# Split down weights kept in device memory: stored at their first use, read back at later ones, in a ring of three pairs

## The reference

```python
x = x + 0.5 * ffn(layernorm(x), ...)
x = x + mamba(layernorm(x), ...)
x = x + 0.5 * ffn(layernorm(x), ...)
# ffn: 8 experts, 128 -> 512 -> 128
h = silu(x @ w_gate[e]) * (x @ w_up[e])
expert_out = h @ w_down[e]
cw = softmax(x @ w_router) * softmax(x @ w_gating / 0.1)
cw = cw / (sum(cw) + 1e-9)
out = sum over e of expert_out[e] * cw[e]
```

## Time and profile before

| | |
|---|---|
| median of 3 runs | 1244.02 us (1243.34 to 1245.47) |
| profiled execution | 1242.44 us, span 1240.6 us |
| granted TensorE clock | 1.00 of full |
| busy: PE, PEld, DVE, ACT, POOL | 1233.1, 1058.2, 1143.4, 1003.6, 446.4 us |
| device memory read, written | 83.30 MB, 2.69 MB |
| DMA moved | 184.84 MB, mean 149 GB/s |

### The profile page before, as it was taken

The page is one execution under the profiler, slowest core; times in us unless marked ns, Lnnn a source line. Parts: engine busy times, 40 slices in busy tenths (PEclk is TensorE's granted clock), DMA queues, the critical chain, the costliest instruction groups (busy, mean ns, idle before and its releaser), DMA issues.

```text
span 1240.6 us, 20186 instructions
## 1 busy us (share of the span) xinstructions
PE 1233.1 (99%) x7072; PEld 1058.2 (85%) x7072; DVE 1143.4 (92%) x1368; ACT 1003.6 (81%) x2122; POOL 446.4 (36%) x571
## 2 busy tenths in 40 slices
PE   9999999999999999999999999999999999999999
PEld 7787788888888888888888888888888888887887
DVE  6958899999999999999999999997999999978877
ACT  7678789798898898988879898797988978846654
POOL 1021134445453463453434434452444344402000
PEclk9999999999999999999999999999999999999999
DMA  8412458888788997987889887986688979932322
GB/s 227 111 27 45 105 116 174 165 171 167 162 176 178 183 187 157 198 170 165 181 180 187 166 196 160 191 181 138 131 166 169 196 169 194 182 63 43 74 48 60
DMA packets 121015, 184.84 MB, mean 149 GB/s; under 512 B 11344, under 2 KB 38096, under 8 KB 120912
## 3 DMA queue, kind: packets, MB, share of 16 engines
q0 software_dynamic: 53568, 97.54, 45.0%
q1 hardware_dynamic: 67344, 86.00, 26.6%
HBM read 83.30 MB, written 2.69 MB: 69 GB/s over the span
## 4 chain that ended last, share of the span: by engine, by line
PE 93%; DVE 3%; ACT 2%; issue 1%; DMA 1%; SPq 0%; DVEq 0%; ACTq 0%
PE PS L1105 28%; PE PS L996 19%; PE PS L999 18%; PE PS L997 18%; PE PS L1101 2%; PE PS L1097 2%; PE PS L1099 2%; PE PS L1163 1%; PE PS L1148 1%; DVE HB L1345 1%; PE PS L1032 1%; DVE HL L1301 1%; PE PS L1040 1%; DMA YE<-CWD 1%; PE PS L1003 0%
## 5 line engine op out<-in xcount | busy, mean ns | idle before, releaser
L1105 PEld LDWEIGHTS PS<-WD,HB 128*128 128x128 f32 x3200 | 393.9, 191 | 22.1 <-issue 2.0
L1105 PE MATMUL PS<-WD,HB 128*128 128x128 f32 x3200 | 395.9, 275 | 0.0
L1345 DVE TENSOR_TENSOR HB<-PS,HB 128x1024 f32<-128x1024 f32 (+1 forms) x336 | 322.9, 962 | 72.5 <-PE PS L999 56.7
L1555 ACT ACTIVATE HB<-PS 128x512 f32<-128x512 f32 x512 | 294.9, 596 | 95.5 <-PE PS L999 93.5
L1733 POOL DMA_DIRECT2D Y<-HS x252 | 221.8, 954 | 317.6 <-DMA Y<-HS 151.7
L996 PE MATMUL PS<-XH,WG 128*128 128x512 f32 x509 | 219.7, 432 | 0.3 <-ACT HB L1555 0.2
L996 PE MATMUL PS<-XH,WU 128*128 128x512 f32 x512 | 204.4, 399 | 0.4 <-DVE HB L1345 0.4
L999 PE MATMUL PS<-XH,WU 128*128 128x512 f32 x512 | 201.2, 393 | 0.0
L999 PE MATMUL PS<-XH,WG 128*128 128x512 f32 x509 | 200.7, 394 | 0.1
L997 PE MATMUL PS<-XH,WU 128*128 128x512 f32 x512 | 200.4, 391 | 0.0
L997 PE MATMUL PS<-XH,WG 128*128 128x512 f32 x509 | 199.3, 392 | 0.0
(11 more groups left out here) (164 smaller groups left out, 1572.9 us busy)
## 6 DMA issues: line engine op xcount, KB each, us to landing
BCB<-BCD SPq DMA_DIRECT2D x128, 512.0 KB, 5.2
Y<-HS POOLq DMA_DIRECT2D x252, 256.0 KB, 6.0
XT<-YE POOLq DMA_DIRECT2D x99, 256.0 KB, 5.1
YE<-CWD SPq DMA_DIRECT2D x27, 256.0 KB, 4.5
AT<-YE POOLq DMA_DIRECT2D x21, 256.0 KB, 3.3
WD<-in_L_ffn_w_down_dram SPq DMA_DIRECT2D x8, 256.0 KB, 6.0
XT<-in_L_attn_x_dram SPq DMA_DIRECT2D x7, 256.0 KB, 5.8
out_dram<-XT SPq DMA_DIRECT2D x7, 256.0 KB, 5.4
```

The costliest lines, as they stand in the source:

```text
L1105: z = pe.matmul(part(g, j), HB[:, i % NH, j * P:(j + 1) * P], WD[:, e, c, :], start=c == 0 and j == 0, stop=c == FC - 1 and j == SUB - 1)
L1345: v.tensor_tensor(H, PS[:, NG + i % 2:NG + i % 2 + n, :], H, ALU.mult).then_inc(S["v_h"], 1)
L1555: a.activation(HB[:, i % NH, :], gate(i), ACT.Silu).then_inc(S["a_sil"], 1)
```

## The change

The 16 pairs that are made for the first time (`MADE`: 10 in position 0, 4 in position 1, 2 in position 14) are still split on ScalarE and VectorE. After the low part, SP stores the split pair, 128 partitions of 2 KB, to a new array `WDD` in device memory (`wd_store`). The 38 later pairs (`READ`) are not split; SP reads them back (`wd_load`) into the ring, which now has three pairs. A read is entered in SP's list when the pair three before it has been multiplied, and after the row loads of experts that come before it. TensorE waits for the read's semaphore instead of those of the two splits. A slot of the ring in which a made pair lies may be written anew only when that pair's store has landed, too.

```diff
+WEIGHTS_RING = 3
+PAIRS_TURNED = [i for i in TURNED_SLOTS if i % PAIR == 0]
+MADE = [i for i in PAIRS_TURNED if not any(k % SLOTS == i % SLOTS for k in PAIRS_TURNED if k < i)]
+READ = [i for i in PAIRS_TURNED if i not in MADE]
...
+    def weight_loads():
+
+        while reads and (asked[0] == len(TURNED) or TURNED[asked[0]] * FC + FC > reads[0] - SPLIT - PAIR - 2):
+            step("wd_load", reads.pop(0))
...
-            if m % PAIR == 0 and m in TURNED_SLOTS:
+            if m in MADE:
                 split_at[m] = split(m)
                 if m not in scalar_splits:
                     step("wd_lo", m, v=.4)
+                    step("wd_store", m)
             m -= 1
             if m in scalar_splits:
                 step("wd_lo", m, after=split_at[m], v=.35)
+                step("wd_store", m)
+            m = nd + SPLIT + PAIR
+            if m in READ:
+                reads.append(m)
             row_loads()
+            weight_loads()
...
-        WDS = sb("WDS", [P, 2, 2, PAIR, P], F32R)
+        WDS = sb("WDS", [P, WEIGHTS_RING, 2, PAIR, P], F32R)
+        WDD = nc.dram_tensor("WDD", [E, FC // PAIR, P, 2, PAIR, P], F32).ap()
...
         def wait_weights_free(eng, i):
-            n = TURNED_SLOTS[i]
-            if n >= 2 * PAIR:
-                eng.wait_ge(S["m_dn"], [k for k in TURNED_SLOTS if TURNED_SLOTS[k] == n - PAIR - 1][0] + 1)
+            n = pair(i) - WEIGHTS_RING
+            if n >= 0:
+                eng.wait_ge(S["m_dn"], PAIRS_TURNED[n] + PAIR)
+                if PAIRS_TURNED[n] in MADE:
+                    wait_weights_stored(eng, PAIRS_TURNED[n])
...
+                elif s[0] == "wd_store":
+                    i = s[1]
+                    wait_weights_high(wt, i)
+                    wt.wait_ge(S["v_wd"], MADE.index(i) + 1)
+                    r = pair(i) % WEIGHTS_RING
+                    sy.dma_start(WDD[i // FC % E, i % FC // PAIR], f32(WDS[:, r])).then_inc(S[f"c_ws{r}"], 16)
+                elif s[0] == "wd_load":
+                    i = s[1]
+                    wait_weights_free(wt, i)
+                    wait_weights_stored(wt, [k for k in MADE if k % SLOTS == i % SLOTS][0])
+                    r = pair(i) % WEIGHTS_RING
+                    sy.dma_start(f32(WDS[:, r]), WDD[i // FC % E, i % FC // PAIR]).then_inc(S[f"c_wl{r}"], 16)
...
-                        wait_weights_high(wt, first)
+                        if first in MADE:
+                            wait_weights_high(wt, first)
+                        else:
+                            wait_weights_read(wt, first)
```

More of the change, by code:

```diff
@@ L445, in row_loads @@
             asked[0] += 1
+    reads = []
+    def weight_loads():
+        while reads and (asked[0] == len(TURNED) or TURNED[asked[0]] * FC + FC > reads[0] - SPLIT - PAIR - 2):
+            step("wd_load", reads.pop(0))
     begun = {"before": 0, "scans": 0, "closing": 0}
@@ L747, in macaron_program @@
             S[n] = ctx.enter_context(nc.semaphore(n))
+        for r in range(WEIGHTS_RING):
+            S[f"c_ws{r}"] = ctx.enter_context(nc.semaphore(f"c_ws{r}"))
+            S[f"c_wl{r}"] = ctx.enter_context(nc.semaphore(f"c_wl{r}"))
         for b in range(BR):
@@ L826, in wait_weights_high @@
             by_scalar = i in scalar_splits
-            same = [k for k in TURNED_SLOTS if k <= i and k % PAIR == 0 and (k in scalar_splits) == by_scalar]
+            same = [k for k in MADE if k <= i and (k in scalar_splits) == by_scalar]
             eng.wait_ge(S["a_wd" if by_scalar else "v_wh"], len(same))
@@ L840, in wait_weights_free, with wait_weights_stored, wait_weights_read @@
         def wait_weights_free(eng, i):
-            n = TURNED_SLOTS[i]
-            if n >= 2 * PAIR:
-                eng.wait_ge(S["m_dn"], [k for k in TURNED_SLOTS if TURNED_SLOTS[k] == n - PAIR - 1][0] + 1)
+            n = pair(i) - WEIGHTS_RING
[3 more added lines that the diff above has]
+                    wait_weights_stored(eng, PAIRS_TURNED[n])
+        def wait_weights_stored(eng, i):
+            r = pair(i) % WEIGHTS_RING
+            eng.wait_ge(S[f"c_ws{r}"], 16 * sum(k <= i and pair(k) % WEIGHTS_RING == r for k in MADE))
+        def wait_weights_read(eng, i):
+            r = pair(i) % WEIGHTS_RING
+            eng.wait_ge(S[f"c_wl{r}"], 16 * sum(k <= i and pair(k) % WEIGHTS_RING == r for k in READ))
         def added(g):
@@ L1091, in _ @@
                     if g in TURNED:
-                        W = WDS[:, pair(i) % 2]
+                        W = WDS[:, pair(i) % WEIGHTS_RING]
                         first = i // PAIR * PAIR
                         high = HI[:, TURNED_SLOTS[i] % HI_RING, :]
-                        wait_weights_high(wt, first)
+                        if first in MADE:
+                            wait_weights_high(wt, first)
+                        else:
+                            wait_weights_read(wt, first)
                         wait_high(wt, i)
                         pe.matmul(turned(g), W[:, 0, c % PAIR, :], high, start=c == 0, stop=False)
-                        wt.wait_ge(S["v_wd"], pair(i) + 1)
+                        if first in MADE:
+                            wt.wait_ge(S["v_wd"], MADE.index(first) + 1)
                         pe.matmul(turned(g), W[:, 1, c % PAIR, :], high, start=False, stop=False)
@@ L1307, in _ @@
                     wt.wait_ge(S[f"c_wd{i // FC % E}"], 16)
-                    v.tensor_copy(WDS[:, pair(i) % 2, 0], WD[:, i // FC % E, c:c + PAIR, :]).then_inc(S["v_wh"], 1)
+                    v.tensor_copy(WDS[:, pair(i) % WEIGHTS_RING, 0], WD[:, i // FC % E, c:c + PAIR, :]).then_inc(S["v_wh"], 1)
                 elif k == "wd_lo":
@@ L1312, in _ @@
                     wait_weights_high(wt, i)
-                    v.tensor_tensor(WDS[:, pair(i) % 2, 1], WD[:, i // FC % E, c:c + PAIR, :], f32(WDS[:, pair(i) % 2, 0]),
+                    v.tensor_tensor(WDS[:, pair(i) % WEIGHTS_RING, 1], WD[:, i // FC % E, c:c + PAIR, :], f32(WDS[:, pair(i) % WEIGHTS_RING, 0]),
                                     ALU.subtract).then_inc(S["v_wd"], 1)
@@ L1571, in _ @@
                     wt.wait_ge(S[f"c_wd{i // FC % E}"], 16)
-                    a.activation(WDS[:, pair(i) % 2, 0], WD[:, i // FC % E, c:c + PAIR, :], ACT.Copy).then_inc(S["a_wd"], 1)
+                    a.activation(WDS[:, pair(i) % WEIGHTS_RING, 0], WD[:, i // FC % E, c:c + PAIR, :], ACT.Copy).then_inc(S["a_wd"], 1)
                 elif k == "acc" and s[1] in scalar_weighs:
```

## The result

| | before | after |
|---|---|---|
| median of 22 runs each, us | 1242.80 (1241.76 to 1245.50) | 1245.26 (1243.11 to 1247.77) |
| profiled execution, us | 1242.44, span 1240.6 | 1243.43, span 1241.3 |

The measured ratio is 1.0017, 95% interval 1.0011 to 1.0023: 2.1 us more, where 1.3 us more was forecast. The two medians themselves lie 2.5 us apart (1.0020). The result is close to the edge of the 0.2% that was called no change. The profiled execution of after is among the quick ones: it lies 1.8 us under its median, that of before 0.4 us under its own.

What follows compares the result with a forecast made beforehand. TensorE, busy 1233.1 of 1240.6 us, was taken as the bound. Position 0 adds 3.0 us, positions 1, 14 and 15 take off 1.7: 1.3 us more, from 1244.0 to 1245.3 us; range 1241.5 to 1249.5.

Steps and rivals of the forecast that it cites:

- What bounds the kernel: Whole kernel: TensorE bounds it, busy 1233.1 of 1240.6 us; VectorE only comes late in places.
- Positions 14 and 15, gain 1.2 us: Last stretch, 1100 to 1234 us: 28 splits go, taking 1.2 us off TensorE's waits.
- Reads at 0: Read pairs land within the 9.4 us the ring allows, so they cost 0, bounds 0 and 1 us.
- Position 0, 3.0 us: About 18 to 66 us: stores in SP's queue delay expert 1's row load; TensorE loses 3.0 us (2.0 to 4.2).
- The steps as listed: Position 0, SP's queue: row load issued 2.0 to 3.2 us later, middle 2.6, plus 0.5 for two transfers ahead.
- Position 1, gain 0.5 us: 90 to 163 us: 0.5 us off; bounds 0.5 us of new waiting and 2.4 us of weight-load waits.
- the middle at 0: 163 to 1100 us: work is kept, only order around the first scans moves; change given as 0.
- Late row loads: Rival, position 0: later row loads also come late, three adding 0.9 to 1.4 us each, 1248.8 us; chance 0.14.
- The freed engines: Rival, last stretch and position 1: VectorE's freed time counts in full, net gain 4.8 us, 1239.2 us; chance 0.11.
- The sign that was to be seen: Position 0: TensorE waits once near 43 us for HL, for over 3 us.
- VectorE's busy time: Sign over the whole kernel: VectorE's busy time falls by about 15 to 17 us, span unchanged.

Runs made afterwards that it cites:

- order kept: The changed kernel, but the planner still books the 38 gone splits, so other steps stay as before: 1241.95 us against 1242.60 before, ratio 0.9995.
- stores only: Against before: all 54 pairs still split, the 16 stores go out, nothing is read back, ring of three pairs: 1243.84 us against 1242.60, ratio 1.0012.
- the kernel with that part alone: Changed kernel without stores in position 0: position 1 makes and stores its pairs, 28 reads in 14 and 15; 1241.83 us against 1242.60 before, ratio 0.9992.
- the four stores alone: Against before: all pairs split, only the first four pairs of position 0 stored, nothing read: 1245.43 us against 1242.71, ratio 1.0016.
- the kernel with the list rearranged: As stores only, with small loads behind the second row load and fourth store behind the first: 1245.25 us against 1243.23 before, ratio 1.0017.
- GpSimd's stores: The changed kernel with its 16 stores issued by GpSimd and not SP: 1248.52 us, ratio 1.0046 against before.
- the kernel with the order kept in 14 and 15 only: The changed kernel with gone splits booked in positions 14 and 15 only, planner free in position 1: 1246.28 us, ratio 1.0024 against before.

## Why the prediction was nearly right in sum and wrong in two terms

In ratios, each against before: the stores cost 0.0012; the gone splits with their reads are worth 0.0017 (from 1.0012 to 0.9995); the moved order costs 0.0022 (from 0.9995 to 1.0017). In us that is +1.5 - 2.1 + 2.7 = +2.1. Each ratio has an interval of 0.0006 to 0.0009 either way, so the terms are good to some 1.1 to 1.6 us. They need not be independent, either: the 11 executions of order kept lie within 1.0 us, those of stores only within 3.3 us, so the quick landing in position 0 may be the rule in the one and not in the other. Of the 2.1 us about 1.0 us would then be positions 14 and 15, and the rest position 0; that is not shown.

- **What bounds the kernel: right.** 13.9 us of VectorE's time went and about 1 to 2 us of TensorE's.
- **Positions 14 and 15, gain 1.2 us: right.** 1.0 to 1.5 us from 1121 to 1230 us in each of the eight traces that have it, 1.0 us by the ratio of the kernel with that part alone.
- **Reads at 0: right.** No matmul waits for one, 2.9 us in the median, 6.4 at most, against the 9.4 us allowed.
- **Position 0, 3.0 us: the mechanism right, the size too large.** The issue came out at 34.75 as counted. The landing was the mis-sized term: 6.89 us plus 0.5 was carried over from before, where the same list now gives 4.9 to 6.5 us. The cost was 0.5 to 3.5 us in five traces, by the ratio of stores only about 1.5 us (2.0 with the four stores alone). The 3 us would have been right only for the bad case, and there about 1 us of it is the lower clock, which the prediction had no term for. The issue, too, hung on more than the count: on CWD's landing. (The steps as listed add to 2.6 + 0.5 = 3.1 us, not 3.0.)
- **Position 1, gain 0.5 us, and the middle at 0: wrong; this step failed.** The runs give 2.7 us of loss for the moved order where the prediction had 0.5 us of gain and 0. It noted that the state-space part starts 2 to 3 slots earlier and gave the bound of 0.5 us of new waiting, looking at VectorE alone. It did not follow the moved step's DMAs: BCD and three BCB transfers go past a row load in SP's list. A warning stood in the trace of before: the one row load that had BCB ahead of it took the 9.6 us of the earlier trace rows, where the median was 4.5 and the other long ones, 6.9 and 8.5, were the two in position 0. With the order kept, position 1 gains next to nothing either (0.3 us in one trace, 0.0 in the other): the wait of 1.20 us at 160.3 us is there with 1.19 us although its first ten pairs are read.
- **The rivals.** Late row loads came, but not at 50 to 65 us, where after has none: one in position 1, and at 57 us in the kernel with the list rearranged. The freed engines did not count in full. The sign that was to be seen, over 3 us of wait for HL near 43 us, was not in after's trace: two waits of 0.47 and 0.23 us were.
- **VectorE's busy time** fell by 13.9 us, under the 15 to 17 us that were to be seen; 19.2 us of splits went, and six more roundings of H at 0.43 us (2.6 us) came back to it.

The forecast of 1.3 us against 2.1 measured is therefore partly luck: 1.5 us too much in one place stood against 2.7 us missed in another. That the forecast median of 1245.3 meets the measured 1245.26 is luck once more: it started from 1244.0, the median of 3 runs, and 22 runs of before have 1242.80. What stays open: why one list gives landings of 4.9 to 6.5 us, and whether the order's cost is the row load, the norm or both.

## What to carry to other kernels

When work is removed from a kernel whose order comes from a planner, book the removed work still, and time that version beside the other: here it was worth some 2.7 us, as much as the removed work itself. Follow each moved step to its transfers and ask which urgent one they now pass in the queue, above all where large ones go out together. A store that nobody waits for still has a place in the queue; put it behind the first transfer that somebody waits for.

## What the runs showed of the hardware

- After TensorE had idled for 2.34, 2.10, 1.94 and 1.59 us, the granted clock was 0.50 (1.2 GHz) for 3.41 us each time, which costs up to 1.7 us beside the wait. After single waits of 1.20 us in before, 1.46 us in the rearranged list and 1.53 us with GpSimd's stores it stayed at 1.00, but so it did after 1.66 us at 41.7 us in the kernel with the order kept in 14 and 15 only. The length of one wait does not decide it alone.
- A row load of 256 KB landed in 4.5 us in the median of before. Behind three transfers of 512 KB that were issued within 1.4 us it took 11.45, 11.79 and 13.09 us with the moved order, and 7.3 to 9.9 us in the traces with the order of before.
- In position 0 the 16 KB store CWD landed 2.5 us after its issue 0.4 us behind a 256 KB store (1.8 us in the rearranged list), and 1.4 us without one; the row load waits for it.
- A store of 256 KB to device memory landed in 2.4 us in the median, no slower than a load of that size (2.9 us). The Trainium skill (DMA: Bandwidth & Descriptors, Anatomy of one DMA), quoted in the prediction, warns of late semaphore updates after such writes; that did not show in the median here. The longest of these 16, 7.5 us, went out at 143.49 us, while the row load behind the BCB transfers was still under way.
